# Self-attention's first quad prepared inside cross-attention's last one, and the causal mask written by quarter products

## The reference

```python
x = x + xattn(_layernorm(x), ctx_1024, ctx_1024, Wq, Wk, Wv, Wo)   # softmax(q k) v @ Wo, no mask used
x = x + attn(_layernorm(x), wq, wk, wv, wo)      # scores/8, causal mask -1e9, softmax, heads, @ wo.T
x = x + ffn(_layernorm(x), W_in, b_in, W_out, b_out)
# ffn: weights rounded to 8 bits by row maxima, activations and hidden to 16 bits by the
# maximum of the whole tensor, exact gelu between the two products
```

## Time and profile before

| What | us |
|---|---|
| median of 3 runs (645.08 to 646.16) | 645.09 |
| the profiled execution | 644.6 |
| its span, first to last instruction | 642.9 |
| cross-attention, start to last instruction | 0 to 288.9 |
| prologue of self-attention, up to the first shift | 289.3 to 310.7 |
| self-attention, first shift to the stage's end | 310.7 to 558.6 |
| feed-forward | 558.9 to 642.9 |

### The profile page before, as it was taken

How to read it: one execution, slowest core, us unless ns; L and a number is a source line. 1 busy time by engine, 2 the same in 40 slices (tenths; PEclk the granted TensorE clock), 3 DMA queues, 4 the chain that set the end, 5 groups by cost and what they waited for, 6 DMA issues and landing times. The chain is left out here.

```text
span 642.9 us, 18565 instructions
## 1 busy us (share of the span) xinstructions
PE 599.8 (93%) x6777; PEld 514.1 (80%) x6777; DVE 470.9 (73%) x978; ACT 383.6 (60%) x1012; POOL 163.4 (25%) x229
## 2 busy tenths in 40 slices
PE   6599999999999999889898999999999999799897
PEld 4588888888888898768697989898989898644597
DVE  4478788888888887768799666666666656677797
ACT  3488788888888888756332333333333333457784
POOL 6524233324342423000211212121212111260400
PEclk9899999999999999999999999999999999999999
DMA  6997867686767767814000000000000000000012
GB/s 197 268 259 183 190 162 182 167 191 168 183 171 185 171 162 206 244 54 140 2 2 2 2 0 0 0 0 0 0 0 0 3 1 2 3 2 0 0 50 83
DMA packets 37037, 58.44 MB, mean 91 GB/s; under 512 B 6912, under 2 KB 15232, under 8 KB 36992
## 3 DMA queue, kind: packets, MB, share of 16 engines
q1 hardware_dynamic: 29328, 42.75, 26.2%
q10 hardware_dynamic: 4592, 8.78, 4.7%
q0 software_dynamic: 3072, 6.30, 4.0%
HBM read 17.96 MB, written 2.10 MB: 31 GB/s over the span
## 5 line engine op out<-in xcount | busy, mean ns | idle before, releaser
L624 ACT ACTIVATE Pr<-pS,nmax 128x256 f32<-128x256 f32 x256 | 120.0, 484 | 27.7 <-DVE nmax L732 27.7
L732 DVE TENSOR_REDUCE nmax<-pS 128x2 f32<-128x512 f32 x128 | 87.4, 684 | 20.2 <-PE pS L468 18.6
L478 PE MATMUL pT<-ident,Pr 128*128 128x128 f32 x512 | 78.1, 275 | 3.3 <-DVE wraw L737 3.1
L966 POOL TENSOR_TENSOR a_Pr<-a_Pr,a_rinv 128x512 f32<-128x512 f32 x32 | 32.7, 1043 | 185.8 <-DVE a_rinv L1277 185.8
L468 PE MATMUL pS<-Kst,Qst 96*128 96x256 f32 x256 | 58.9, 312 | 12.1 <-DMA Qst<-QSl 6.8
L1147 ACT ACTIVATE a_Pr<-a_Pr 128x512 f32<-128x512 f32 x32 | 20.2, 631 | 76.0 <-DVE a_Pr L1269 76.0
L478 PEld LDWEIGHTS pT<-ident,Pr 128*128 128x128 f32 x512 | 59.6, 141 | 4.6 <-issue 4.2
L468 PEld LDWEIGHTS pS<-Kst,Qst 96*128 96x128 f32 x256 | 40.2, 193 | 20.9 <-issue 10.0
L624 ACT ACTIVATION_READ_ACCUMULATOR Pr<-pS,nmax 128x1 f32 x256 | 55.0, 215 | 0.0
L287 POOL DMA_DIRECT2D Qst<-QSh x60 | 30.2, 506 | 80.5 <-PE pS L468 56.3
L59 PE MATMUL a_pJ<-a_XTh,a_W1h 128*128 128x256 f32 x128 | 37.1, 290 | 2.5 <-DVE X L1290 1.6
(11 more groups left out here) (323 smaller groups left out, 1974.6 us busy)
## 6 DMA issues: line engine op xcount, KB each, us to landing
Kst<-WO_ints SPq DMA_DIRECT2D x96, 128.0 KB, 3.1
CT<-ctxT ACTq DMA_DIRECT2D x16, 512.0 KB, 4.8
Kst<-KSh SPq DMA_DIRECT2D x62, 128.0 KB, 3.1
Qst<-QSh SPq DMA_DIRECT2D x64, 64.0 KB, 2.3
Qst<-QSh POOLq DMA_DIRECT2D x64, 64.0 KB, 2.9
Kst<-KSl SPq DMA_DIRECT2D x31, 128.0 KB, 3.3
Qst<-QSl SPq DMA_DIRECT2D x32, 64.0 KB, 2.2
Qst<-QSl POOLq DMA_DIRECT2D x32, 64.0 KB, 2.9
```

Of the source, the lines that this page charges most:

```text
L478: last = pe.transpose(pT[s % 2][:, t, k, :], Pr[s % 2][:, t, P * k:P * k + P], ident[:, :])
L624: act.activation(Pr[c % 2][:, t, :], pS[c % 2][:, t, :], ACT.Exp, bias=nmax[c % 2][:, t:t + 1], accum_out=rsum[par][:, c // 4, 2 * (c % 4) ...
L732: dve.tensor_reduce(nmax[s % 2][:, :], pS[s % 2][:, :, :], AX.X, ALU.max, negate=True).then_inc(maxed, 1)
L966: pool.tensor_tensor(rows, rows, rinv[s][:, :].unsqueeze(2).to_broadcast([P, 8, SQ]), ALU.mult).then_inc(weighted, 1)
```

## The change

It does these things:

- Both stages share tensors (`Shared`): self-attention's Wq, Wk, Wv in high and low lie in cross-attention's CS, KS, QS and Kst buffers, its Wo high in Qst, its QT in CT, its KT in raw[:, 0].
- `steps` writes out all eight bodies in both attention stages.
- In cross-attention, body 6 also takes the statistics of "quad 8", which is tiles 0 and 1 again, and normalises them; the last body has eleven events instead of two (LAST): X, two V, four Q fills and four K fills of self-attention's quad 0 (the last of them after the loop, in place of keep_busy). ACT copies one half of each, DVE the other.
- The splits of Wq, Wk, Wv and the high part of Wo are POOL's, at the end of its stream in cross-attention; the low part of Wo is POOL's at the start of self-attention. ACT and DVE have none.
- Self-attention has no prologue but the statistics and norm of quad 1.
- The mask of a bank is written by two products of 64x64x512, so four for a tile.
- `load_later` is issued in another order; the loads of the feed-forward weights no longer wait for splits, and W_out has a buffer of its own.
- At the start POOL issues its half of the first Q restack before it computes rstd of quad 1, and ACT loads the context of pair 2 after its seventh copy and not after its fourth.
- In feed-forward the next group's transposes move behind f=3, and its high and low parts behind f=4.

```diff
@@ class Shared (new)
+        cs = [[t[:, :, :].rearrange("p k n -> p (k n)") for t in pair] for pair in self.CS]
...
+        self.W = [[cs[0], ks], [qs, cs[1]], [quarter[:2], quarter[2:]]]
+        self.WO_high = self.Qst[:, :, :, :, :, :].rearrange("p j r g a q -> p (j r g a q)")
...
@@ cross_attention
+        LAST = {0: ("X", 2, 0), 2: ("V", 1, 0), 3: ("V", 1, 1), 4: ("SQ", 2, 0), 6: ("SQ", 2, 1), 7: ("SQ", 2, 2),
+                8: ("SQ", 2, 3), 10: ("SK", 2, 0), 12: ("SK", 2, 1), 14: ("SK", 2, 2), 16: ("SK", 2, 3)}
+        BEFORE_LAST = EV0 + EV * (QUADS - 1)
...
         def steps(eng, body):
-            body(0, False)
-            with eng.Fori(1, QUADS - 2) as i:
-                body(i, False)
-            body(QUADS - 2, False)
-            body(QUADS - 1, True)
+            for i in range(QUADS):
+                body(i, i == QUADS - 1)
...
@@ sync
                     if late:
-                        load_later(0)
+                        load_later(1)
                     restack_k(sp, 1, EV0 + EV * i + 8, CHUNKS * (2 * i + 2))
                     restack_q(sp, qst_sync[1], 1, EV0 + EV * i + 3, CHUNKS * (2 * i + 2), (0, 1))
+                    if i == QUADS - 3:
+                        load_later(0)
                     if late:
-                        for m in range(1, 4):
-                            load_later(m)
+                        load_later(2)
+                        load_later(3)
@@ gpsimd
+            restack_first_q(pool, qst_in[0], (2, 3))
             rstd_of(1)
-            restack_first_q(pool, qst_in[0], (2, 3))
...
+            def split_high(m):
+                pool.wait_ge(raw_in[m], 16)
+                for k in range(KC):
+                    pool.tensor_copy(shared.W[m][HI][k], raw[:, m, HE * k:HE * k + HE]).then_inc(weights_high, 1)
...
             steps(pool, body)
+            pool.wait_ge(proj, BEFORE_LAST)
+            split_high(0)
+            pool.wait_ge(kst_in[0], RESTACK * QUADS)
+            split_low(0)
+            for par in range(2):
+                q_restacked(pool, par, QUADS)
+            apart(pool, waited)
+            split_high(1)
+            pool.wait_ge(proj, BEFORE_LAST + 3)
+            split_low(1)
+            pool.wait_ge(scores, CHUNKS * (PAIRS - 1))
+            split_high(2)
+            split_low(2)
+            pool.wait_ge(raw_in[3], 16)
+            pool.tensor_copy(shared.WO_high, raw[:, 3, :])
@@ tensor
+                elif kind in ("SQ", "SK"):
+                    m = ("SQ", "SK").index(kind)
+                    pe.wait_ge(lo, BEFORE_LAST + 1)
+                    pe.wait_ge(weights_split, m + 1)
+                    for t in range(2):
+                        j = 2 * part + t
+                        last = split_matmul(pe, bank[:, 256 * t:256 * t + 256], shared.weights(m, slice(P * j, P * j + P)),
+                                            parts(XT))
...
             weigh(QUADS - 1, 12, True)
-            keep_busy(pe, 5, pJ[0][:, :], identb, causal)
+            r, k, kind, ahead, part = event(QUADS - 1, 16, True)
+            project(r, pJ[k % 2], r - 1, kind, part, PAIRS, 0)
             turn_o(PAIRS - 1)
-            keep_busy(pe, 3, pJ[0][:, :], identb, causal)
             turn_back(PAIRS - 1)
-            keep_busy(pe, 5, pJ[0][:, :], identb, causal)
             project_out(PAIRS - 1)
@@ scalar
                 if r == 3:
                     split_w(W_ORDER[3])
+                if r == 6:
                     load_ctx(2, 0, 1)
@@ self_attention, gpsimd
-            rstd_of(0)
             rstd_of(1)
+            flat = "p j d -> p (j d)"
+            pool.tensor_tensor(WO[LO].rearrange(flat), raw[:, 3, :], f32(WO[HI]).rearrange(flat), ALU.subtract
+                               ).then_inc(wo_split, 1)
@@ tensor
                 for b in range(2):
-                    pe.matmul(pS[2 * t + b][:, :], identb[:, :], causal[:, :, :], start=True, stop=False,
-                              skip_group_check=True)
+                    for side in range(2):
+                        rows, half_bank = slice(SQ * ((side + b) % 2), SQ * ((side + b) % 2) + SQ), slice(SQ * side, SQ * side + SQ)
+                        pe.matmul(pS[2 * t + b][half_bank, :], identb[rows, rows], causal[rows, :, :],
+                                  start=True, stop=False, skip_group_check=True)
@@ feed_forward
-                    if f == 1 and not last:
+                    if f == 3 and not last:
                         turn(g + 1)
...
-                    if f == 2 and not last:
+                    if f == 4 and not last:
                         x_high(g + 1)
```

More of the change, by code:

```diff
@@ L113, in hold, with statistics_of @@
         self.turned, self.bias_in, self.bias_out = turned, bias_in, bias_out
[L116 removed]
+def statistics_of(dve, stats, mv, X, quad, stats_done, mv_done, waited, first=0):
     for t in range(2):
@@ L250, in event @@
         def event(i, c, last):
+            if last:
+                if c not in LAST:
+                    return None
+                k = list(LAST).index(c)
+                return BEFORE_LAST + k, k, *LAST[c]
             if c not in EVENTS:
@@ L604, in high @@
                     act.activation(V[ahead % 2][:, 2 * part, :], bank[:, 0:D], ACT.Copy).then_inc(hi, 1)
+                elif kind in ("SQ", "SK"):
+                    heads = shared.QT if kind == "SQ" else shared.KT
+                    act.activation(heads[2 * part], bank[:, 0:256], ACT.Copy).then_inc(hi, 1)
                 elif kind == "Q":
@@ L691, in _ @@
             take_even(PAIRS - 1)
+            r, k, kind, ahead, part = event(QUADS - 1, 16, True)
+            high(r, pJ[k % 2], kind, ahead, part, QUADS - 1)
             o_high(PAIRS - 1)
@@ L829, in _ @@
             merge(PAIRS - 1)
+            r, k, kind, ahead, part = event(QUADS - 1, 16, True)
+            low(r, pJ[k % 2], kind, ahead, part, QUADS - 1)
             scale_o(PAIRS - 1)
@@ L959, in rstd_of @@
             def rstd_of(n):
-                rstd_of_quad(pool, vare, rstd, mv, half, n, ln_mv, ln_ve, ln_rs, waited)
+                rstd_of_quad(pool, vare, rstd, mv, half, n, ln_mv, ln_ve, ln_rs, waited, 1)
             def divide(i, s):
@@ L1001, in bank_read @@
                     done, order = (by_act, BY_ACT) if (kind, part) in BY_ACT else (by_dve, BY_DVE)
-                    pe.wait_ge(done, len(order) * quad + order.index((kind, part)) + 1)
+                    pe.wait_ge(done, len(order) * quad + order.index((kind, part)) + 1 - AHEAD)
             def fill(bank, kind, part, quad):
```

210 lines of the change are left out of this document (100 added, 110 removed).

## The result

The changed kernel takes **635.39 us** at the median of 5 runs (634.37 to 638.59) against 646.05 (645.08 to 646.25) for the kernel before beside it: a ratio of 0.9844, interval 0.983 to 0.9858. The sign was right, the size too large: 629.0 was forecast, with 624.5 to 634 as the range. The profiled execution is the run of 638.59, with a span of 636.8.

What follows compares the result with a forecast made beforehand. PE, busy 93% of the span, was taken as the bound, with room in cross-attention's last quads. Terms -18.45 + 6.2 - 1.4 - 1.9 - 0.4 = -16.0 took the profiled 644.6 to 628.6, median 629.0 us; range 624.5 to 634.

Steps and rivals of the forecast that it cites:

- Cost 0: Start of self-attention: POOL's low part of Wo, 4.7 us, makes the first division at most 0.1 late, so costs nothing.
- Prologue: Between cross- and self-attention: of 21.78 us only a 3.3 us norm chain remains, so 18.45 us are removed.
- Last quads: End of cross-attention: the added statistics, transposes and fills cost +6.2 us, partly hidden in PE's waits; bounds +3 and +10.
- All is hidden: Last quads: POOL's weight splits come in time, with 2.6 us to spare at first use and 3 at step 10.
- the rival of a late POOL: Last quads: at twice their length POOL's splits have Wk ready at 282.3, some 3.5 us late: 632.5 us; chance 8%.
- Mask: Self-attention's scores: four quarter products run beside each other, 0.33 us instead of 0.53, 0.2 saved seven times: -1.4 us.
- the serial rival: Mask: quarter products run one after the other, 633.6 us, or only the halves of one bank do, 630.4; chance 12%.
- brings nothing: Mask of a quad's second score: it lies beside DVE's shifts and sums, for which PE then waits 0.49 us; no gain.
- Feed-forward: Transposes two column blocks later remove PE's waits of 1.24 and 0.89 us: -1.9 us, between 0 and -2.1.
- Start: Kernel's start: POOL's earlier half of the first Q restack removes a wait of 1.48 us, little kept: -0.4 us.
- The bound of +1: Upper end of the start's range, -1.5 to +1 us, since the later context load lies beside the Q restack.
- Loops: Writing out all quads of both attention stages: nothing to gain or lose, 0, as looped and written-out self-attention quads take 32.03 and 32.02.

Runs made afterwards that it cites:

- e1: Changed kernel with POOL's subtraction for Wo's low part made to wait for the normalization of quad 1: 629.95 us, ratio 0.9766.
- e9: Changed kernel with POOL's subtraction for Wo's low part moved behind the four divisions of self-attention's first quad: 632.63 us, ratio 0.9792.
- e11: e9 with 5, 3 and 5 padding products back in the last pair's tail, and a wait for DVE's last low part: 632.49 us, ratio 0.9789.
- e3: Changed kernel with the mask written again by two 128x512 products for each score instead of eight 64x512 ones: 638.54 us, ratio 0.9883.
- e2: Changed kernel with both edits of the start undone (POOL's order of rstd and Q restack, ACT's context load): 634.58 us, ratio 0.9824.
- e7: e1 with both edits of the start undone: 630.99 us, ratio 0.9758.
- e10: e9 with the context load of pair 2 back behind the fourth projection, POOL's new order kept: 632.26 us, ratio 0.9778.
- e15: e9 with POOL's old order at the start (rstd ahead of the Q restack), the late context load kept: 631.12 us, ratio 0.9774.
- e4: Kernel before with only the loops over quads of both attention stages written out: 647.11 us, ratio 1.002.
- e16: e9 with both edits of the start undone, all quads of cross-attention written out: 629.72 us, ratio 0.9767.
- e17: e9 with both edits of the start undone and cross-attention's quads 1 to 4 in a loop again: 629.88 us, ratio 0.9767.
- e12: The same kernel as e17, run earlier: 629.77 us, ratio 0.9746.

## Why the prediction was right and wrong

**The step that failed is "Cost 0" for POOL's low part of Wo.** It asked only whom POOL's 4.7 us would delay on POOL itself, the divisions; it did not ask which DVE work runs beside it. Measured: 4.25 us at the first shift, and 3.7 at the median, if the changed kernel's 635.4 is set against the mean of e1, e9 and e11 (631.7), which differ from it in that step (e11 in its padding too) and among themselves by 2.7.

The trace of the kernel before had the effect already. Timeline of DVE, kernel before:

```profile
10.39 1.56 DVE L727 TENSOR_SCALAR XN<-X,mv,rstd 128x256 f32<-128x256 f32 x2 [0.94 <-POOL rstd L385]
```

This is the same kind of normalisation. One of its two instructions takes 1.23 us instead of 0.41 and ends some 0.15 us behind POOL's cast of 10.77 to 11.81. A mean over all of the line's instructions hides it.

Point by point, against the table:
- *Prologue.* Removed as forecast; with the split moved, all profiles have the first shift 3.32 to 3.35 us behind cross-attention's end, where 3.3 was forecast. The step itself was right.
- *Last quads.* 47.7 forecast, 48.15 in most profiles and up to 48.84: right to 0.5 in most, with some luck. The half quads are 15.66 and 16.85 (15.5 and 17.3 forecast), but step 10 to the end of the last weigh takes 12.0 where 11.3 was forecast. Body 6's statistics cost 0.43 (15.84 to 16.27), not 0.75. No wait of PE on POOL's splits appears: "All is hidden" was right. (In the rival of a late POOL, 282.3 would be 4.0 us behind step 10 at 278.3, not 3.5; nothing hangs on it.)
- *Mask.* The four products do run beside each other; the serial rival is out, and with it the rule of the Trainium skill (TensorEngine Tiling (Array Packing), "Gotcha 1: PSUM Pressure") as it was weighed: by it 0.53 us would have stayed, 0.24 are measured. The size was under: -1.4 was put, 0.2 a quad; 0.40 a quad is measured, -2.6 in e3's profile and -3.2 by its median. The part of it that failed is that score(1) "brings nothing", since one mask is only 0.29 shorter; and 0.33 for the four was 0.24.
- *Feed-forward.* -1.9 forecast. The rest is 4.37 us shorter than before, of which e3 gives 2.47 to the mask: -1.9; undone on e1 it is 2.35. Right within 0.5.
- *Start.* -0.4 forecast. Undoing it lowers the ratio by 0.0020 (e2) and 0.0008 (e7), 0.5 to 1.3 us, the second within the scatter; what the runs show is no gain, and first merges that scatter to the late side. The bound of +1 had named one possible cause, the later context load; e10 and e15 don't single it out.
- *Loops.* 0 forecast; 0.6 to 1.9 us by e4, nothing in the pair e16 and e17. The loop's quad and the static one that were compared lie in self-attention, where no DMA runs (share 0.00 and 0.01), and there nothing changed in e4 either; in cross-attention, where the share is 0.75, only body 6 was looked at, and the late half quad is quad 5's.
- *Clock.* No term was given to it, though the change takes away 39 padding products. Every changed kernel shows one drop or more between the last quads' tail and the first 12 us of quad 0, where the kernel before shows none; in quad 0 it costs 0 to 1.2 us. e11 puts 13 of them back and wins nothing.

The sum by the changed kernel's second profile: 631.7 is the forecast's 627.0 with +4.3 (gap), +0.6 (middle), +0.6 (quad 0), +0.5 (last quads), -0.2 (start), -1.0 (rest, that is mask and feed-forward). Its execution took 633.48; the median is 1.9 above that, which is scatter of the start and the clock that these runs bound but don't divide. With the failed step taken away and the start undone, the kernel takes 629.7 to 631.0 us (e7, e12, e16, e17), where 629.0 was forecast. Part of that closeness is luck: the mask's surplus of 1.2 pays for what the middle and the last quads lack.

## What to carry to other kernels

Work moved to an idle engine is free only if the engines that it shares something with are free as well: for each SBUF-to-SBUF operation of POOL, look at which forms DVE runs beside it (here the `tensor_scalar` grew, sums and reciprocals didn't), and expect the record to show a longer busy time, not a wait. Look at the longest instruction of a line, not only at the mean: the kernel before had one of 1.23 us among those of 0.41. Where the DMA share is near 1, as at the start here, an edit that only reorders issues should be given a spread and not a gain. Profile a changed kernel twice before explaining a stage: the first profile here put 4 us on a start that the second didn't have.

## What the runs showed of the hardware

- Four bf16 products of 64x512 on different quarters of the array, two to each PSUM bank, begin within 0.01 us of each other, and the next product begins 0.24 us behind the first of them; behind the first of two products of 128x512 it begins at 0.53.
- A pair of DVE `tensor_scalar` instructions from SBUF to SBUF, 0.73 us alone, takes 4.98 beside a POOL subtraction of 4.56 us, and the profile shows it as busy. Beside the same subtraction DVE's sum over SBUF (0.68) and reciprocal (0.20) don't grow.
- One drop of the granted clock to its lower level costs quad 0 nothing (34.83 to 34.86 us) where it has ended by 2 us behind the first shift, and 1.2 us (36.00 to 36.06) where it lies 8 to 12 us behind it; 13 padding products ahead of it gained nothing.
